# Second attention: sums made by the mixing products, inverses spread by transfers, and another order of the step

## The reference, cut to what matters

```python
q = (x @ Wq).reshape(b, n, 32, 16)
k, v = jnp.split(ctx @ Wkv, 2, axis=-1)          # both reshaped to 32 heads of 16
q = apply_axial_rope(q, pos_map); k = apply_axial_rope(k, ctx_pos_map)
logits = jnp.einsum('bqhd,bkhd->bhqk', q, k) * scale
w = jax.nn.softmax(logits, axis=-1)
attn = jnp.einsum('bhqk,bkhd->bqhd', w, v).reshape(b, n, 512)
x = x + attn @ Wout + bout
```

## Time and profile before

| what | value |
|---|---|
| device time, median of 3 runs | 1957.01 us (1955.76 to 1959.29) |
| device time of the profiled execution | 1958.99 us |
| its span in the trace | 1957.2 us |
| TensorE busy / VectorE busy, whole span | 98% / 67% |
| granted TensorE clock, mean of the core | 0.995 |
| second attention, loop and tail | about 1085 to 1425 us of the span |

### The profile page before, as it was taken

How to read it: one execution, slowest core, us unless ns; L and a number is a source line. 1 busy time by engine, 2 the same in 40 slices (tenths; PEclk the granted TensorE clock), 3 DMA queues, 4 the chain that set the end, 5 groups by cost and what they waited for, 6 DMA issues and landing times. The chain is left out here.

```text
span 1957.2 us, 35844 instructions
## 1 busy us (share of the span) xinstructions
PE 1911.5 (98%) x13296; PEld 1540.1 (79%) x13296; DVE 1321.1 (67%) x2493; ACT 733.9 (37%) x2275; POOL 556.7 (28%) x705
## 2 busy tenths in 40 slices
PE   6999999999999999999999899999999999999999
PEld 5788888778888878888888677777688888888887
DVE  6666666765665654334263699998768787888786
ACT  5555545654555542111121445444433222122211
POOL 4323322322224335101021334343210223222221
PEclk9999999999999999999999899999999999999999
DMA  6553333543355442201032200000121645655554
GB/s 207 135 150 79 91 73 85 152 109 99 99 137 146 104 121 90 76 11 54 11 98 75 64 20 26 19 21 30 42 92 54 193 158 196 206 194 166 193 168 159
DMA packets 157015, 205.62 MB, mean 105 GB/s; under 512 B 23537, under 2 KB 111601, under 8 KB 156913
## 3 DMA queue, kind: packets, MB, share of 16 engines
q1 hardware_dynamic: 133200, 117.26, 21.6%
q0 software_dynamic: 23712, 87.04, 13.7%
HBM read 136.61 MB, written 17.30 MB: 79 GB/s over the span
## 5 line engine op out<-in xcount | busy, mean ns | idle before, releaser
L2387 POOL DMA_INDIRECT m_ring<-in_table,m_row x128 | 125.6, 981 | 372.0 <-DVE l_x_all L2500 272.0
L48 PE MATMUL four_banks<-l_yT_hi,m_hi 128*128 128x512 f32 x512 | 199.4, 390 | 0.0
L48 PE MATMUL four_banks<-l_yT_lo,m_hi 128*128 128x512 f32 x512 | 199.2, 389 | 0.0
L533 ACT ACTIVATE prob<-four_banks,mx,rms 128x128 f32<-128x128 f32 x256 | 121.6, 581 | 171.4 <-DVE mx L671 171.4
L1149 DVE TENSOR_SCALAR f_relu<-bank,f_b 128x512 f32<-128x512 f32 x64 | 48.0, 749 | 163.6 <-ACT f_h_hi L1092 163.6
L1092 ACT ACTIVATE f_h_hi<-bank,f_b 128x512 fp32r<-128x512 f32 x64 | 44.1, 689 | 257.2 <-PE bank L48 257.2
L335 POOL TENSOR_TENSOR rms<-ssq,constants 128x4 f32<-128x4 f32 x128 | 27.2, 213 | 394.9 <-ACT junk_k L521 277.3
L338 POOL TENSOR_TENSOR rms<-rms,constants 128x4 f32<-128x4 f32 x128 | 129.8, 1014 | 10.0
L48 PEld LDWEIGHTS four_banks<-l_yT_hi,m_hi 128*128 128x128 f32 x512 | 96.1, 188 | 20.3 <-issue 0.2
L48 PEld LDWEIGHTS four_banks<-l_yT_lo,m_hi 128*128 128x128 f32 x512 | 96.1, 188 | 19.7
L2364 ACT ACTIVATE m_act_of<-m_dot,l_ln_y 128x2 f32<-128x2 f32 x64 | 18.9, 296 | 239.6 <-DVE m_junk L2490 239.6
(11 more groups left out here) (314 smaller groups left out, 5286.9 us busy)
## 6 DMA issues: line engine op xcount, KB each, us to landing
qkT<-blocks SPq DMA_DIRECT2D x256, 128.0 KB, 2.7
pT_sb<-dealt SPq DMA_DIRECT2D x256, 64.0 KB, 2.1
f_stage<-in_w POOLq DMA_DIRECT2D x14, 512.0 KB, 4.6
f_x_in<-x SPq DMA_DIRECT2D x18, 256.0 KB, 3.1
ctx_in<-in_ctxT SPq DMA_DIRECT2D x32, 128.0 KB, 2.6
x_in<-in_x SPq DMA_DIRECT2D x16, 256.0 KB, 3.2
x<-xres SPq DMA_DIRECT2D x16, 256.0 KB, 2.8
x<-l_x_all SPq DMA_DIRECT2D x16, 256.0 KB, 2.1
```

The lines of the kernel that those rows point to most:

```text
L48: mm = pe.matmul(out, st, mv, start=first and n == 0, stop=last and n == len(terms) - 1)
L533: a = act.activation(prob[g][:, j, :].rearrange("q (b a) -> q a b", b=4), scores, ACT.Exp, bias=mx[g][:, 1, j:j + 1], scale=rms[g][:, 0, j ...
L2387: pool.indirect_dma_start(ring[slot][:], None, table, bass.IndirectOffsetOnAxis(ap=row[:, tile_of(g), k:k + 1], axis=0)).then_inc(S[f"got{ ...
```

## The change

`sum_up` and the tile `ones` go. `v_sb` is filled with ones and not zeros, each head's values stand in the first 16 of its 32 columns, and `mix` makes odd and even heads apart: 16 products for f = 1 into bank 6, then 16 for f = 0 into bank 7. Of each 32 rows of a bank, 16 are mixed values and 16 are the head's sum. ScalarE copies both banks to SBUF (`o_in`, tile `mixed_sb`). SyncE moves the sums (one row out of 32, 4 rows of 4 KB) into `sums`, a tile of 128x32, which VectorE inverts; the inverses go to a DRAM tensor and come back by one transfer that repeats each of its 8 rows 16 times into 128 rows of 2 KB (256 KB), into `rotB[1]`'s place. Four transfers of 16 rows of 2 KB each bring the odd heads beside the even ones. `normalise` is then one product of two SBUF tiles.

The order within a step changes on every engine. TensorE's list becomes: keys(s+1), shifted scores (s, 0), turn_q(s+1, 0), turn_y(s-2), queries(s+2), turn_k(s+1, 0 and 1), shifted scores (s, 1), turn_q(s+1, 1), values(s+1), score(s+1, 0), output(s-1), score(s+1, 1), mix(s), turn_x(s+3). Values go to bank 4; transposed input and most of turn_y go to bank 5.

```diff
@@ sync
+        def move_sums(s):
+            sp.wait_ge(*at("o_in0", s))
+            sp.dma_start(sums[:], mixed_sb[D:P:PAD].rearrange("j f x -> j (f x)")).then_inc(S["sums_moved"], 16)
+        def move_odd(s, blocks):
+            for j in blocks:
+                sp.dma_start(mixed_sb[PAD * j + D:PAD * (j + 1), 0, :], mixed_sb[PAD * j:PAD * j + D, 1, :]).then_inc(S["o_moved"], 16)
+        def move_outputs(s):
+            sp.wait_ge(S["sums_moved"], 48 * s + 16)
+            move_odd(s, (0, 1))
+            sp.wait_ge(*at("inv_ready", s))
+            sp.dma_start(inverses.rearrange("j f (c x) -> (j f c) x", x=32), sums[:]).then_inc(S["sums_moved"], 16)
+            if there(s + 2):
+                sp.wait_ge(*at("roped1", s + 2))
+            move_odd(s, (2, 3))
+            sp.wait_ge(S["sums_moved"], 48 * s + 32)
+            sp.dma_start(spread_inv, inverses.rearrange("j f x -> (j f) x").unsqueeze(1).to_broadcast([8, D, DM])
+                         ).then_inc(S["sums_moved"], 16)
         def step(s):
+            if there(s - 1):
+                move_sums(s - 1)
+            if there(s) and not (isinstance(s, int) and s == 0):
+                move_maxima(s, 1)
+            if there(s - 1):
+                move_outputs(s - 1)
             if there(s + 2):
                 load_ctx(sp, s + 2)
+            if there(s + 1):
+                move_maxima(s + 1, 0)
             if there(s - 1):
                 store(s - 1)
...
-            if there(s + 1):
-                move_maxima(s + 1, 0)
-                move_maxima(s + 1, 1)
@@ tensor
     def mix(pe, s):
         pe.wait_ge(*at("v_copied", s))
...
-    def sum_up(pe, s):
         pe.wait_ge(*at("exped1", s))
         if there(s - 1):
             pe.wait_ge(*at("y_added", s - 1))
...
+        for f in (1, 0):
...
+            for t in range(4):
+                for j in range(4):
+                    mm = pe.matmul(bank[(7, 6)[f]][PAD * j:PAD * (j + 1), t * P:(t + 1) * P], v_sb[:, 8 * t + 2 * j + f, :],
+                                   probT[f][:, j, t, :], start=True, stop=True)
+            mm.then_inc(S[f"mixed{f}"], 1)
@@ scalar, step: new places
             if there(s + 2):
                 copy_qk(act, s + 2, 0)
             if there(s + 1):
                 turned_in(act, s + 1, 1, 0)
             if there(s):
                 exps(act, s, 1)
...
                 turned_in(act, s + 1, 0, 1)
             if there(s - 1):
                 o_hi(act, s - 1)
             if there(s + 1):
                 turned_in(act, s + 1, 1, 1)
...
+            if there(s):
+                o_in(act, s, 1)
+                o_in(act, s, 0)
@@ vector
     def invert(dve, s):
-        dve.wait_ge(*at("summed", s))
-        dve.reciprocal(rden[:], bank[6][:]).then_inc(S["rden_ready"], 1)
+        dve.wait_ge(S["sums_moved"], 48 * s + 16)
+        dve.reciprocal(sums[:], sums[:]).then_inc(S["inv_ready"], 1)
     def normalise(dve, s):
-        dve.wait_ge(*at("rden_ready", s))
-        dve.wait_ge(*at("mixed", s))
-        if there(s - 1):
-            dve.wait_ge(*at("oT_lo", s - 1))
-        dve.tensor_tensor(o_sb[:], bank[7][:], rden[:], ALU.mult).then_inc(S["o_ready"], 1)
+        dve.wait_ge(S["o_moved"], 64 * (s + 1))
+        dve.wait_ge(S["sums_moved"], 48 * (s + 1))
+        dve.tensor_tensor(o_sb, o_sb, spread_inv, ALU.mult).then_inc(S["o_ready"], 1)
```

More of the change, by code:

```diff
@@ L1602, in sum_up @@
             pe.wait_ge(*at("k_copied", s + 1))
-        for f in range(2):
-            for j in range(4):
-                mm = pe.matmul(bank[6][PAD * j:PAD * (j + 1), :], ones[:, D * (1 - f):D * (3 - f)],
-                               probT[f][:, j, :, :].rearrange("p t q -> p (t q)"), start=f == 0, stop=f == 1)
-        mm.then_inc(S["summed"], 1)
+        for f in (1, 0):
+            if f == 0 and not there(s + 1):
+                pe.wait_ge(*at("o_in0", s - 1))
+            for t in range(4):
[3 more added lines that the diff above has]
+            mm.then_inc(S[f"mixed{f}"], 1)
     def output(pe, s):
@@ L1682, in step @@
         def step(s):
+            last = isinstance(s, int) and s == NB - 1
             if there(s + 1) and not (isinstance(s, int) and s == 0):
@@ L1686, in step @@
                 score_shifted(pe, s, 0)
-            if there(s - 1):
-                output(pe, s - 1)
             if there(s + 1):
@@ L1692, in step @@
                 turn_y(pe, s - 2)
-            if isinstance(s, int) and s == NB - 1:
+            if last:
                 turn_y(pe, SHORT)
+            if there(s + 2):
+                queries(pe, s + 2)
+            if there(s + 1):
+                turn_k(pe, s + 1, 0)
+                turn_k(pe, s + 1, 1)
             if there(s):
                 score_shifted(pe, s, 1)
-            if isinstance(s, int) and s == NB - 1:
+            if last:
                 turn_y(pe, SHORT + 1)
@@ L1700, in step @@
             if there(s + 1):
-                turn_k(pe, s + 1, 0)
-            no_queries = isinstance(s, int) and s == NB - 2
-            if there(s + 2):
-                queries(pe, s + 2)
-            if no_queries:
                 turn_q(pe, s + 1, 1)
-                turn_k(pe, s + 1, 1)
+                values(pe, s + 1)
+                score(pe, s + 1, 0)
+            if there(s - 1):
+                output(pe, s - 1)
             if there(s + 1):
-                score(pe, s + 1, 0)
-                if not no_queries:
-                    turn_k(pe, s + 1, 1)
-            if there(s):
-                sum_up(pe, s)
-            if there(s + 1):
-                if not no_queries:
-                    turn_q(pe, s + 1, 1)
-                values(pe, s + 1)
                 score(pe, s + 1, 1)
@@ L1835, in step @@
         def step(s):
-            if there(s - 1):
-                o_hi(act, s - 1)
             if isinstance(s, int) and s == NB - 1:
@@ L2073, in step @@
                 rope(dve, s + 1, 0)
+            if there(s + 2):
+                x_lo(dve, s + 2)
+            if there(s - 2):
+                layer_norm_y(dve, s - 2)
             if there(s + 1) and not (isinstance(s, int) and s == 0):
                 by_sine(dve, s + 1, 1)
-            if there(s + 2):
-                x_lo(dve, s + 2)
+            if there(s - 1):
+                invert(dve, s - 1)
             if there(s + 1):
                 rope(dve, s + 1, 1)
+            if turned_here(s - 2):
+                y_lo(dve, s - 2)
+            if isinstance(s, int) and s == NB - 1:
+                y_lo(dve, SHORT)
             if there(s + 2):
                 copy_cosines(dve, s + 2)
+            if there(s + 3):
+                layer_norm(dve, s + 3)
+            if there(s + 2):
+                by_sine(dve, s + 2, 0)
+            if there(s + 4):
+                statistics(dve, s + 4)
+            if there(s - 1):
+                normalise(dve, s - 1)
+            if isinstance(s, int) and s == NB - 1:
+                y_lo(dve, SHORT + 1)
+            if there(s + 1):
+                maxima(dve, s + 1, 0)
             if there(s - 1):
@@ L2121, in vector @@
         chain[0] = 0
+        invert(dve, NB - 1)
+        normalise(dve, NB - 1)
+        layer_norm_y(dve, NB - 2)
         ahead["vector"](dve, 1)
```

137 lines of the change are left out of this document (63 added, 74 removed).

## The result

| | before | after |
|---|---|---|
| device time, median of 6 runs each | 1957.03 us (1955.76 to 1959.29) | 1964.92 us (1959.89 to 1965.77) |
| profiled execution, its span | 1958.99, 1957.2 us | 1959.89, 1958.1 us |
| granted TensorE clock, mean | 0.995 | 0.989 |

The ratio is 1.0036, 95% interval 1.0023 to 1.0049: slower by 0.4%, where 1936 us was forecast. The profiled execution of after was the quickest of its six. The trace therefore explains why nothing was gained, and not all of the 7.9 us between the medians.

What follows compares the result with a forecast made beforehand. TensorE (20.09 of 20.41 us a step) was the bound, VectorE close behind; new step 18.8. Loop -22.9, start -3.4, block 14's step +0.1, block 15's +3.0, tail +0.6, weights +1.0: -21.6, so 1936 us, range 1928 to 1948.

Steps and rivals of the forecast that it cites:

- TensorE's work: Loop step: 1.85 us of ones products and a 0.32 us wait go, from 20.41 to a floor of 18.24.
- VectorE's sum: VectorE's busy time in a loop step falls from 18.69 to about 15.7 us, mainly through a smaller reciprocal.
- block 14 to 15: Block 15's step, with little work to hide the chain behind, goes from 15.34 to 18.3 us, +3.0.
- The rule weighed against the change: `normalise`, now with two SBUF inputs, can be locked out by GpSimd reading SBUF; without it 0.1 us less a step.
- VectorE's list up to `layer_norm_y`: Loop step: VectorE's work from the end of the output products through `layer_norm_y` (about 0.5 us) ends at 6.2 us.
- the transfers: Loop step: inverses leave at 9.4, transfer back issued at 10.85, takes 3.2, lands at 14.05; output starts at 15.65 us.
- the signs that the prediction names for being wrong: Output waits over 1 us a step, `normalise` starts later than 15 us, or the score waits for a late shifted row.
- Sums and maxima behind the weights: Step 13: the sums and second maxima stand behind the last stage's weight loads, +1.0 us.
- After the last mixing: Tail: 8.3 us from the mixing's end to the output products become a chain of 9.1, +0.6 us in the sum.
- The start: Step 0: ones products and a wait for the first exponentials go, second score waits for first maxima; about -3.4 us.
- the transfer back is slower: Rival, 24%: with 8 source rows the transfer back lands in 4.0 us, not 3.2; 0.75 a step, +10, 1946 us.
- 90% for "faster": Chance of over 0.2% (3.9 us) faster: own case 42% (1931 to 1941 us) plus rivals of 24, 12 and 12%.

Runs made afterwards that it cites:

- its second run: The kernel after, run once more with nothing altered: median 1964.19 us, ratio 1.0023 to the kernel before.
- the run with 16 rows: Against the kernel after, inverses written twice to DRAM so the transfer back has 16 source rows repeated 8 times, not 8 repeated 16 times: 1972.65 us, ratio 1.0075.
- The best versions: Kernel after with weights loaded earlier and transfer back ahead of an odd move: 1950.98 us; plus `layer_norm_y` ahead of `x_lo` everywhere: 1950.28; in the loop alone: 1951.65.

## Why the prediction was wrong

**What held.** TensorE's work (1.85 us of products gone; floor forecast 18.24, measured 18.36 once nothing waits), VectorE's sum (15.7 forecast, 16.06), ScalarE's (10.9 against 10.50), the small reciprocal (0.3, was 0.34), and block 14 to 15 (+3.0, was +3.44). There the chain held link by link: counted from the end of the output products, the inverse at 9.1 us (forecast 9.5), `normalise` at 14.5 (14.1), the end of the output at 18.9 (18.6). TensorE's waits of 1.14 and 1.96 us in that step were not forecast, and cost little only because the chain was longer. The rule weighed against the change had no occasion: `normalise` took 0.69 us, and GpSimd's `root` had ended before it began.

**The step that failed first: VectorE's list up to `layer_norm_y`.** Counted from the end of the output products, at about 1185.25, `layer_norm_y` was to end at 6.2 and ended at 7.5. It was costed 0.5 us; it took 1.32. Another 0.49 us went ahead of `rope`, where VectorE waited for nothing that the profile shows; block 13's step, which is not in the hardware loop, does not have that gap. I priced GpSimd's interference on `by_sine` (2.87) and forgot the instruction ahead of it: `by_sine` in fact took 1.84, since only one GpSimd operation ran across it. For the inverse the errors nearly cancel, which is luck: the reciprocal ended at 9.55, forecast 9.35. For the turning on TensorE they do not: it waited 0.92 us. With that wait TensorE's own list reached the end of the score at 16.3 and not 15.5, so that without the transfers too the step measured 19.20 us, and not 18.8. The Trainium skill, "SBUF — State Buffer", "Who interferes with whom", lists `tensor_scalar`, which this operation is (a subtraction and a product with two scalars, from SBUF to SBUF), among those that can take the shared ports for the whole instruction; it excepts them from its rule that one SBUF input does not contend. The prediction gives that rule without the exception. The rows agree with the exception: 1.32 us beside `by_cosine`, 0.54 to 0.55 without it.

**The terms that were mis-sized: the transfers.** The mechanism was right and was named as a rival. The inverses' write went out at 9.6 (forecast 9.4). The transfer back was to leave at 10.85 and left at 11.4, because the odd moves take 0.6 us each and not 0.4, and two do not fit under the write's flight. It was to take 3.2 and took 4.11, close to the rival's 4.0. So `normalise` began at 15.5 and not 14.05, and the output at 16.9 and not 15.65. The output started 1.25 us late, and the step came out 1.07 us longer than forecast (13.9 over 13 steps). Of the signs that the prediction names for being wrong, `normalise` later than 15 us came true; the output's wait of over 1 us a step did not (0.57). Taking the transfers of the inverses away gives back 0.6 of it, since the other wait then sets the step.

**Two steps of the tail.** Sums and maxima behind the weights were costed at 1.0 us together, without following them to TensorE. But the sums themselves were late, and with them the inverse and, on VectorE's list behind it, `rope` of the keys. So TensorE waited 3.30 us for `l_roped`, and its next products ran at the low clock. Moving the load took 3.9 us out of that step: 1.3 of waiting, the rest TensorE's busy time (16.02 us for 18.56, with a clock of 0.91 for 0.77). After the last mixing I forecast 9.1 us of chain (set against the 8.3 of before that is +0.8, where the sum has +0.6) and it was 12.3 (1406.0 to 1418.33): sums 2.07 for 1.6, two odd moves of 1.15 that I had under a flight, the inverses' write 3.35 for 1.5, the way back 3.49 for 3.2. In the run with the odd moves in another place the write left at 1404.32 with no move ahead of it and had landed when the way back left at 1405.89, 1.57 us later: so the moves ahead of it were what made it slow. The order alone gave 2.1 us back.

**What was not in the sum at all: the clock.** The earlier trace rows have 1.00 everywhere, and I costed every product at full clock. The new waits of 1 to 4 us are followed by stretches at 1.2 GHz: +1.85 us in the last output here, about 2 us in the first of the 13 steps, 1.6 to 1.9 us in single steps of two other runs. Whether this also makes the median of after lie 5 us over its own profiled execution stays open: only one execution of a run has a trace, and the mean clocks of its second run do not order the times (0.990 both at 1958.39 and at 1964.90 us).

**The start** gained 2.05 us and not 3.4: ahead of its last scores there TensorE waited 2.50 us for the maxima, a wait that the forecast names without a price of its own.

**Of the rivals**, "the transfer back is slower" named what happened: it was priced at 4.0 us and 0.75 a step, measured 4.11, and the run with 16 rows bears out the reason it gives. It was priced with everything else unchanged. The prediction itself says that three lists end within 0.2 us of each other and that small errors mostly make the step longer; the mistake behind 90% for "faster" was to give the range 0.35 us either way all the same. For the end result the tail alone was +12.6 of losses against 4.7 forecast.

What stays open: how much of the remaining 0.7 to 1.1 us a step over the floor could be won without leaving the transfers out. The best versions have 1950 to 1952 us, 0.3% to 0.4% faster than before, and lie too close together to be ranked.

## What to carry to other kernels

When work is taken from the engine that is full, the new bound need not be another engine: here it was a chain of waits through several. Write the chain link by link, count every issue of the queue that stands between two links, and put the transfer that something waits for ahead of those that nobody wants yet: here two places in one list were worth 13 us of 1964. In the last steps, where little work lies beside, a chain shows in full, and bulk loads do not belong ahead of its small transfers. Two waits of one step can hide each other, so one of them removed alone says little (0.6 and 0.5 us here, 1.5 together); remove both in one experiment.

## What the runs showed of the hardware

- A transfer from SBUF to SBUF of 32 KB costs 0.52 to 0.6 us of SyncE's time and lands in 1.9 us; right behind one of 256 KB it takes 3.3.
- 256 KB spread from 8 rows of DRAM take 4.1 us from issue to use in the loop, from 16 rows 3.6.
- An instruction of VectorE with one input in SBUF took 1.32 us beside one of GpSimd, and 0.54 to 0.55 without it.
- TensorE's granted clock fell after waits of only about 1 us in some steps and not in others: 0.63 us a product after 1.09 of waiting, 0.40 after 1.11. A step with such a fall is 1.6 to 1.9 us longer. The Trainium skill, "TensorE: Matmul & The Clock Gate", "HAM oscillation — how this bites in real kernels", describes such falls where products wait for transfers again and again. The runs agree in that, but the waits of its example are longer ones, and here about 1 us was at times enough.
- With extra products in the waits of the last steps the granted clock rose from 0.77 and 0.82 to 0.92, and the time stayed (1964.36 and 1964.19 us); how much of a gain their own time covers is not shown.
